# A shared mixture of experts on Trainium2: the order of a pass's products on TensorE, and of copies and powers on GpSimd

## What is computed

```
shared = silu(x @ sh_up_w + sh_up_b) @ sh_down_w + sh_down_b
scores = softmax(x @ gate_w.T)              # 8 experts
topk_w, topk_i = top_k(scores, 2)
topk_w = topk_w / (sum(topk_w) + 1e-20)
comb = sum over the two of one_hot(topk_i) * topk_w
h = silu(x @ up_w[e] + up_b[e])             # 128 x 128 for each expert e
y = sum over e of comb[e] * (h @ down_w[e] + down_b[e])
result = y + shared
```

## Time and profile before

| | us |
|---|---|
| median of 3 runs | 1112.68 |
| lowest, highest run | 1112.1, 1117.41 |
| the profiled execution | 1110.67 |
| its span in the profile | 1108.6 |
| TensorE busy | 990.0 (89%) |
| VectorE busy | 786.0 (71%) |
| ScalarE busy | 556.0 (50%) |
| GpSimd busy | 237.1 (21%) |

### The profile page before, as it was taken

How to read it: one execution, slowest core, us unless ns; L and a number is a source line. 1 busy time by engine, 2 the same in 40 slices (tenths; PEclk the granted TensorE clock), 3 DMA queues, 4 the chain that set the end, 5 groups by cost and what they waited for, 6 DMA issues and landing times.

```text
span 1108.6 us, 33395 instructions
## 1 busy us (share of the span) xinstructions
PE 990.0 (89%) x12437; PEld 794.8 (72%) x12437; DVE 786.0 (71%) x1908; ACT 556.0 (50%) x1068; POOL 237.1 (21%) x248
## 2 busy tenths in 40 slices
PE   4779999979999997899989999988999989989887
PEld 4558888857777776678858877766878867656646
DVE  6776877576777776556397577748677667887877
ACT  2543433655556553343455655545565653455543
POOL 4661221122222221332010000000000002255300
PEclk9899999999999998999999999999999999999989
DMA  9300000000000000000000000000000000000001
GB/s 360 156 1 1 0 0 0 1 2 2 1 0 0 0 0 2 1 1 1 1 2 1 0 0 0 1 2 2 0 0 0 0 3 1 1 1 1 0 1 39
DMA packets 5926, 16.23 MB, mean 15 GB/s; under 512 B 729, under 2 KB 4962, under 8 KB 5218
## 3 DMA queue, kind: packets, MB, share of 16 engines
q1 hardware_dynamic: 5858, 15.29, 3.5%
HBM read 14.24 MB, written 1.05 MB: 14 GB/s over the span
## 4 chain that ended last, share of the span: by engine, by line
PE 60%; DVE 13%; issue 13%; DVEq 8%; ACT 3%; POOL 2%; POOLq 1%; ACTq 0%
PE banks L1829 9%; PE banks L1902 5%; PE banks L1874 5%; PE banks L1536 4%; PE banks L974 3%; PE banks L1862 3%; PE banks L1231 3%; PE banks L1579 2%; PE banks L1890 2%; PE banks L1451 2%; PE banks L1653 2%; PE banks L1566 1%; PE banks L375 1%; PE banks L1619 1%; PE banks L2364 1%
## 5 line engine op out<-in xcount | busy, mean ns | idle before, releaser
L1837 ACT ACTIVATE work<-banks 128x512 f32<-128x512 f32 x128 | 74.9, 600 | 70.6 <-PE banks L1829 70.6
L364 POOL TENSOR_TENSOR rstd<-var,nhalf 128x2 f32<-128x2 f32 x64 | 44.9, 702 | 299.3 <-DVE var L335 291.8
L1432 ACT ACTIVATE work<-work 128x1024 f32<-128x1024 f32 x64 | 67.9, 1060 | 43.2 <-DVEq L1428 25.7
L1829 PE MATMUL banks<-xT_all,weights 128*128 (+1 forms) x384 | 86.2, 380 | 2.3 <-ACT work L1951 1.8
L1985 DVE TENSOR_TENSOR work<-banks,neg_mask 128x512 f32<-128x512 f32 x64 | 40.7, 685 | 62.0 <-PE banks L1862 60.6
L1829 PEld LDWEIGHTS banks<-xT_all,weights 128*128 128x128 f32 x384 | 71.5, 190 | 13.7 <-ACT work L1951 2.6
L1012 ACT ACTIVATE work<-banks,weights 128x256 f32<-128x256 f32 x128 | 53.5, 472 | 54.6 <-PE banks L964 53.7
L1458 ACT ACTIVATE work<-banks 128x512 f32<-128x512 f32 x128 | 68.0, 604 | 11.4 <-PE banks L1451 7.7
L1902 PEld LDWEIGHTS banks<-weights,work 128*128 128x128 f32 x512 | 58.4, 191 | 14.8 <-ACT work L1951 14.8
L974 PE MATMUL banks<-weights,work 128*128 128x128 f32 x512 | 63.1, 276 | 5.5 <-DVE work L1113 5.0
L974 PEld LDWEIGHTS banks<-weights,work 128*128 128x128 f32 x512 | 60.9, 191 | 9.7 <-ACT work L1012 8.3
(11 more groups left out here) (350 smaller groups left out, 2286.4 us busy)
## 6 DMA issues: line engine op xcount, KB each, us to landing
weights<-wpack SPq DMA_DIRECT2D x1, 5381.5 KB, 32.3
weights<-wpack SPq DMA_DIRECT2D x1, 2060.0 KB, 13.4
weights<-wpack SPq DMA_DIRECT2D x1, 2049.0 KB, 17.6
weights<-wpack SPq DMA_DIRECT2D x1, 1160.5 KB, 19.9
x_all<-x_in SPq DMA_DIRECT2D x2, 512.0 KB, 4.8
ctxT_all<-ctxT_in SPq DMA_DIRECT2D x1, 1024.0 KB, 7.3
out<-x_all SPq DMA_DIRECT2D x8, 128.0 KB, 1.8
rows<-rows_in SPq DMA_DIRECT2D x1, 832.0 KB
```

Source lines behind the costliest of these rows:

```text
L1432: act.activation(sm[:, u, :], sm[:, u, :], ACT.Exp, scale=scale).then_inc(h["exp"].sem, 1)
L1829: ins = pe.matmul(bank(ring.bank(f"qk{c}"))[:, j * PT:(j + 1) * PT], wt[:, 2 * (c % 4) + j, :], cols(src, p), start=True, stop=True)
L1837: act.activation(dst.rearrange("p c t -> p (c t)"), bank(ring.bank(f"qk{c}")), ACT.Copy) \
```

## The change

TensorE's pass begins with up0; the router product of the next pair follows it, then up1 and up2, the transposes of the mixture weights, up3 and up4. ScalarE's copy of the turned weights stands between the Silus of up2 and those of up3. The units of a pass are named in the new order, so each takes another bank. On GpSimd the copy for pair 1 stands ahead of the power of pair 0, and the copy for pair 2 ahead of the power of pair 1.

```diff
--- before.py
+++ after.py
@@ -264,8 +264,8 @@
         ups5 = [(f"up{j}", "a") for j in range(5)]
         spreads4 = [(f"b{g}", "v") for g in range(4)]
         moe1.pro = stage([("route", "v")], 1)
-        moe1.body = stage([("route", "v"), ("combT", "a")] + ups5 + spreads4, PAIRS - 1)
-        moe1.epi = stage([("combT", "a")] + ups5 + spreads4, 1)
+        moe1.body = stage(ups5[0:1] + [("route", "v")] + ups5[1:3] + [("combT", "a")] + ups5[3:5] + spreads4, PAIRS - 1)
+        moe1.epi = stage(ups5[0:3] + [("combT", "a")] + ups5[3:5] + spreads4, 1)
 
         def opened():
 
@@ -1213,24 +1213,31 @@
                                             start=False, stop=(e == 7))
                     ins.then_inc(y_filled, 1)
 
+                def up(ring, i, p, j):
+                    settle(pe)
+                    pe.wait_ge(*ring.bank_free(i, f"up{j}"))
+                    bk = bank(ring.bank(f"up{j}"))
+                    for c in range(2 * j, min(2 * j + 2, 9)):
+                        ins = pe.matmul(bk[:, (c % 2) * PT:(c % 2 + 1) * PT], upw[:, c, :], cols(xT_all, p),
+                                        start=True, stop=True)
+                    ins.then_inc(banks_filled, 1)
+
                 def part(ring, i, p, k, loop=False):
+                    up(ring, i, p, 0)
                     if ring is s.body:
+                        settle(pe)
                         route(pe, ring, i, p + 1)
-                        settle(pe)
+                    up(ring, i, p, 1)
+                    up(ring, i, p, 2)
+                    settle(pe)
                     pe.wait_ge(*comb_ready.at(p, 1))
                     pe.wait_ge(*ring.bank_free(i, "combT"))
                     for u in range(2):
                         ins = pe.transpose(bank(ring.bank("combT"))[:, u * P:(u + 1) * P],
                                            comb4[:, u, :, :].rearrange("p g e -> p (g e)"), ident[:])
                     ins.then_inc(banks_filled, 1)
-                    for j in range(5):
-                        settle(pe)
-                        pe.wait_ge(*ring.bank_free(i, f"up{j}"))
-                        bk = bank(ring.bank(f"up{j}"))
-                        for c in range(2 * j, min(2 * j + 2, 9)):
-                            ins = pe.matmul(bk[:, (c % 2) * PT:(c % 2 + 1) * PT], upw[:, c, :], cols(xT_all, p),
-                                            start=True, stop=True)
-                        ins.then_inc(banks_filled, 1)
+                    up(ring, i, p, 3)
+                    up(ring, i, p, 4)
                     pe.wait_ge(*ring.emptied(i, "combT"))
                     for g in range(4):
                         settle(pe)
@@ -1262,9 +1269,11 @@
                 act.preload_act_table(ACT.Silu)
 
                 def part(ring, i, p, k, loop=False):
-                    act.wait_ge(banks_filled, ring.filled(i, "combT"))
-                    act.activation(combT4[k], bank(ring.bank("combT"))[:, 0:PT], ACT.Copy).then_inc(act_emptied, 1)
                     for j in range(5):
+                        if j == 3:
+                            act.wait_ge(banks_filled, ring.filled(i, "combT"))
+                            act.activation(combT4[k], bank(ring.bank("combT"))[:, 0:PT], ACT.Copy) \
+                                .then_inc(act_emptied, 1)
                         act.wait_ge(banks_filled, ring.filled(i, f"up{j}"))
                         for c in range(2 * j, min(2 * j + 2, 9)):
                             ins = act.activation(hidden[k][:, c, :],
@@ -2937,11 +2946,11 @@
                     pending = (s, None)
                     continue
                 if s is moe1:
+                    stage_inputs(g, s, 1)
                     prog[s][3](g, 0)
-                    stage_inputs(g, s, 1)
                     take_last(g, (pending[0], None))
+                    stage_inputs(g, s, 2)
                     prog[s][3](g, 1)
-                    stage_inputs(g, s, 2)
                     prog[s][3](g, 2)
                     with g.Fori(2, PAIRS - 1) as p:
                         stage_inputs(g, s, p + 1)
```

## The result

| | before | after |
|---|---|---|
| median, us | 1114.54 (1112.1 to 1119.73, 9 runs) | 1109.0 (1107.55 to 1110.93, 9 runs) |
| ratio | | 0.9945, 95% interval 0.993 to 0.9961 |
| the profiled execution, us | 1110.67 | 1110.93 |

What follows compares the result with a forecast made beforehand. TensorE was taken as the bound, with 60% of the chain. 4.6 us from passes 0 and 1 plus 0.6 from later passes make 5.2, so 1112.7 becomes 1107.5 us; range 1104.0 to 1111.3.

Steps and rivals of the forecast that it cites:

- Passes 0 and 1: Shared mixture's first two passes, ahead of its loop: TensorE's four waits go, pass 1's spreads start 4.6 us earlier.
- the 0.3 allowed: Sign of being right: TensorE has no wait over 0.3 us for GpSimd's queue or L1316 in passes 0 and 1.
- the gap behind the drain: TensorE behind the router product, in the sums for passes 0 and 1: reckoned with 0.50 us.
- the transposes: TensorE's transposes of the mixture weights, in the sum for pass 0: reckoned with 0.43 us.
- The clock's 1.3 us: Pass 1's nine products took 5.35 us instead of 4.05 at lowered clock; filling the stretch saves some 1.3 us.
- The later passes: Passes behind the first two: transposes and jump back cost less, 0.6 us in all, bounds 0 and 1.0.
- added waits: New waits on VectorE, ScalarE and banks; ScalarE's copy ends 0.3 us before up4, so its wait costs nothing.
- rival C: L1266, all eight passes: the copy of the turned weights delays the spreads 0.9 us each; 1114.9 us, chance 0.06.
- The 0.6 us of small gains: Later passes: 0.4 us from transposes in four passes and some 0.2 at the jump back.
- Banks: ... all of them emptied microseconds before: TensorE's products each wait for another predecessor in their ring, all emptied microseconds before.
- rival B: Clock gives more: the fall from 1059.4 to 1066.2 goes, saving 1.8 to 2.5 us further; 1105.4 us, chance 0.19.

Runs made afterwards that it cites:

- e5: The kernel before with unused wide products added in TensorE's two long waits; 1108.13 us, ratio to before 0.9955.
- e2: The changed kernel with GpSimd's copies put back behind the powers, new order kept on TensorE and ScalarE; 1111.13 us, ratio to before 0.9972.
- e3: The kernel before with only GpSimd's copies moved ahead of the powers, TensorE and ScalarE in the old order; 1114.51 us, ratio to before 1.0016.
- e1: The changed kernel without the wait for the copy of the turned weights ahead of the spreads' four bank waits; 1105.66 us, ratio to before 0.993.
- e6: e1 with the drain behind the router product replaced by an increment on up1's first product; 1104.9 us, ratio to before 0.9931.
- e11: The kernel before with six idle semaphore increments of TensorE ahead of the stage's first router product; 1113.37 us, ratio to before 1.0009.
- e12: e6 with seven idle semaphore increments of TensorE ahead of the stage's first router product; 1104.28 us, ratio to before 0.9918.

## Why the prediction came out as it did

**Passes 0 and 1: right, term by term.** 4.6 us forecast, 4.64 measured, with copies where they were reckoned and weights 0.23 us behind the point at which TensorE wanted them, within the 0.3 allowed. Some terms erred against each other: the gap behind the drain was 0.26 outside the loop and 0.39 inside, not 0.50, the transposes 0.22, not 0.43, and the wait ahead of pass 0's spreads took this back. The clock's 1.3 us were right for this trace (e5: 5.35 to 4.05).

**The two parts.** The order alone gives pass 0 and 1.6 us by pass 1, with a fall of the clock left in it (e2); the copies alone only rename the waits (e3); together they give the 4.64. The forecast reckoned them as one, which was right.

**The later passes: wrong.** The step that failed is the one on added waits: "So 0.3 us are to spare and I cost the wait at nothing." The times in it were right to 0.05 us. What it left out is what is queued behind the waiting instruction on its own engine: four increments with four bank waits, and in the loop three computations between them, which run while up3 and up4 are busy when nothing holds them (e1). The spreads came 0.90 us behind the copy's end (0.88 to 0.91 in passes 2 to 5, 0.60 in 6 and 7), and the stage lost 2.8 by it (91.26 less 88.44). It is rival C at its place, through another mechanism and under its price of 0.9 a pass. The 0.6 us of small gains were there (0.85 in e1). A smaller step failed too, "Banks: ... all of them emptied microseconds before": in pass 0 the router's bank was emptied only 0.46 us before the spreads started, and TensorE stood for 0.56 us, once. Nothing was run that takes this wait alone away, but in e6, where TensorE comes 0.4 us sooner, the spreads start at 5.52 again and the wait is 0.96. With e1 the stage gains 5.49 where the forecast had 5.2.

**The sum: right in part by luck.** The stage gave 2.7 where 5.2 was forecast; that the runs came near the forecast all the same is not the mechanism's doing. The means of the timed runs differ by 4.3 us. 2.1 of it is time at full clock. The traces show about as much: 1.4 in the stage (2.7 less 1.3 for the clock) and 1.0 to 1.6 in pass 7 of the next stage, less some 0.7 in that stage's pass 0 (24.2 to 24.4 before, 25.0 after), which also differed between repeats of one kernel. The other 2.2 is half of 4.4 us less low clock. 1.3 of that is the fall in pass 1. The remaining 0.9 is low clock at other places, rival B in kind, and can be chance: by the spread of the runs I estimate the 4.4 uncertain by 3. No trace ties it to the falls near the end, where the three traces of before have 3.4 to 6.8 us of low clock and the two of after 3.4 and 6.8. Why the filled kernel meets so little low clock stays open too: e5 lost 7.3 us of it, and one fall of 3.4 is what it removes in its own stage.

The Trainium skill (TensorE: Matmul & The Clock Gate, "Part 1: The HAM clock gate") says that TensorE's activity is judged in windows that run free of the kernel. From this the prediction took that some runs of before would have no fall in pass 1, so that the change would gain 1.3 us less in them. No trace bears that out: all five in the old order with the thin stretch of pass 1 unfilled (three of before, e3, e11) have the fall there. What differs between them is its length, 3.4 or some 6.8 us, as the rule would allow; the windows themselves no trace shows.

## What to carry to other kernels

Ahead of a wait that you move close to its cause, look at what stands behind it in its own queue: satisfied waits and increments behind an unsatisfied one cost their full issue time once it is met (here 0.60 to 0.90 us). Put the wait that is met last at the end of its group, and drop it where another asks for the same count. To judge a gain of half a per cent, compare stages in several traces and count the low clock apart; medians alone can credit an edit with what the place of later code or a filled idle stretch gave.

## What the runs showed of the hardware

Code can cost time by its place. TensorE stood 1.43 us without a releaser in the middle of 128 products of 0.018 us each, in the kernel before, and 0.88 in e6; six more instructions ahead of them and it did not. The Trainium skill, Runtime: NRT & Kernel Launch, section "Instruction fetch mechanics", says that each engine fetches its instructions in blocks of 256 and that crossing into the next is mostly hidden. The traces bear the first out. The page of before counts the fetches, packets of 16384 bytes on the queue of instructions:

```profile
q8 instruction: 47, 0.77, 0.3%
```

One of them starts at 726.69, 0.83 us behind the start of the small products, and the gap ends 2.54 us later, at 729.23; in e6 it is 721.38 and 723.64. In after, e11 and e12, which have no gap there, one starts 2.1 to 6.8 us ahead of the products. In all 14 traces together, 70 gaps of over 0.6 us without a named wait stand inside such groups of 64x64 products behind 500 us, 4 to 6 in each. Every one ends 2.2 to 2.8 us after the start of such a packet, and the two that before has at 756.68 and 760.84 stand exactly 256 of TensorE's recorded instructions apart in every trace that has both. That the crossing is mostly hidden holds as well: in before 27 packets start behind 500 us, and 5 of them stand ahead of such a gap. Among very short products it wasn't hidden. Which engine a packet is for, the trace doesn't say.

One wait held up four increments, with the waits that they carry, until it was met. Outside the loop they started 0.15 us apart and the spreads came 0.60 us behind the copy's end; in the loop, with a computation of 0.03 us between each two (L1244), they started 0.24 to 0.27 apart and it was 0.90. A wait without such a queue behind it is quicker: before's transposes start at 455.37, 0.05 us after VectorE's last step (455.09 + 0.23). In pass 6 of the changed kernel the copy ends at 520.80 and the spreads start at 521.40:

```profile
L384 PEldq EVENT_SEMAPHORE  x4: 51/51/51, 520.8 to 521.3; - x4
```

```profile
521.40 1.15 PE L1248 MATMUL banks<-free 32*128 32x256 f32 x16 [0.23 <-issue]
```
